# An AdaLN transformer block with attention and a routed feed-forward part on one core: order of weight loads, row stores, ranking and the first feed-forward batch's preparation

## The reference, cut to what matters

```python
def attn(x, Wq, bq, Wk, bk, Wv, bv, temperature):      # b=8, t=1024, d=512, 16 heads of 32
    q = (x @ Wq + bq).reshape(b, h, dh, t)             # k and v alike
    attn = softmax(einsum('bhdt,bhds->bhts', k, v) * temperature)
    return einsum('bhdt,bhts->bhds', q, attn).reshape(b, t, d)

def ffn(hidden, w_router, W1, b1, W2, b2):             # F = 2048
    scores = einsum('bsd,d->bs', hidden, w_router)
    top_scores, top_idx = top_k(scores, 512)           # half of the 1024 tokens of a batch
    selected = take_along_axis(hidden, top_idx)
    processed = gelu(selected @ W1 + b1) @ W2 + b2
    return hidden.at[top_idx].add(sigmoid(top_scores) * processed)

sa, ca, ga, sb, cb, gb = (silu(c) @ wmod) split in six  # |ga|, |gb| at least 0.25
h = layernorm(x) * (1 + ca) + sa
x = x + ga * attn(h, ...)
h = layernorm(x) * (1 + cb) + sb
x = x + gb * ffn(h, ...)
```

## Time and profile before

| what | value |
|---|---|
| profiled execution, own time | 2431.43 us |
| its span | 2429.7 us |
| median of the timed runs | 2440.17 us |
| PE busy | 2272.0 us (94%) |
| DVE busy | 1903.2 us (78%) |
| ACT busy | 1477.5 us (61%) |
| POOL busy | 1367.7 us (56%) |

### The profile page before, as it was taken

One profiled execution on the slowest core, in us unless ns is written; L12 is line 12 of the kernel. 1 busy time (PEld: TensorE's weight loads), 2 busy tenths in 40 slices (PEclk: granted clock), 3 DMA queues, 4 the chain that ended last, 5 costly groups with the idle time before them and its releaser, 6 DMA issues.

```text
span 2429.7 us, 41301 instructions
## 1 busy us (share of the span) xinstructions
PE 2272.0 (94%) x12772; PEld 886.5 (36%) x12772; DVE 1903.2 (78%) x2806; ACT 1477.5 (61%) x2616; POOL 1367.7 (56%) x1205
## 2 busy tenths in 40 slices
PE   7999999999999999999999999877689999999996
PEld 2333333333333333333333333222244444444443
DVE  5899999999999999999999999988444543553432
ACT  1788888888888888878888888767211111111110
POOL 4566676667666666667666675553344452443531
PEclk9999999999999999999999999999899999999998
DMA  6233333232333334233333334223312012011100
GB/s 212 69 91 78 78 87 85 68 96 67 81 95 75 74 77 101 68 79 83 79 81 90 77 71 101 64 60 110 108 44 66 22 48 62 28 61 44 54 25 18
DMA packets 123771, 180.83 MB, mean 74 GB/s; under 512 B 44112, under 2 KB 44112, under 8 KB 123480
## 3 DMA queue, kind: packets, MB, share of 16 engines
q1 hardware_dynamic: 113760, 152.30, 25.0%
q0 software_dynamic: 9728, 25.23, 3.4%
HBM read 67.17 MB, written 43.16 MB: 45 GB/s over the span
## 4 chain that ended last, share of the span: by engine, by line
PE 65%; DVE 16%; issue 9%; POOL 4%; ACT 3%; DMA 1%; SPq 1%; DVEq 0%; POOLq 0%; ACTq 0%
PE sc L552 13%; PE sc L741 13%; PE acc L599 13%; PE sc L728 12%; DVE nmax L976 9%; PE pj L562 8%; PE pj L574 5%; POOL x L1314 3%; DVE qn L1037 2%; ACT probs L804 2%; DVE stats L1019 1%; PE sc L585 1%; PE sc L614 1%; DVE rinv L1032 0%; DMA room<-in_L_ffn_W 0%
## 5 line engine op out<-in xcount | busy, mean ns | idle before, releaser
L804 ACT ACTIVATE probs<-sc,nmax 128x1024 f32<-128x1024 f32 x1024 | 1136.7, 1115 | 272.5 <-DVE nmax L976 254.8
L976 DVE TENSOR_REDUCE nmax<-sc 128x1 f32<-128x1024 f32 x1024 | 1212.1, 1215 | 57.0 <-PE sc L552 51.4
L599 PE MATMUL acc<-probs,qn 128*32 128x512 f32 x4136 | 554.6, 609 | 3.3 <-DVE qn L1037 2.3
L878 ACT ACTIVATE probs<-sc,b_col 128x512 f32<-128x512 f32 x128 | 87.8, 687 | 552.2 <-PE sc L728 552.1
L562 PE MATMUL pj<-room 128*128 128x512 f16 x1536 | 395.3, 381 | 0.4 <-ACT qT L794 0.4
L741 PE MATMUL sc<-room,probs 128*128 128x512 f16 x1536 | 354.7, 381 | 26.8 <-DVE probs L1165 26.8
L552 PE MATMUL sc<-room 128*128 128x512 f16 x1024 | 309.4, 384 | 40.7 <-ACT probs L804 24.1
L552 PE MATMUL sc<-stacks 128*128 128x512 f16 x1024 | 309.6, 384 | 38.3 <-ACT probs L804 37.7
L1163 DVE CAST probs<-probs 128x512 f16<-128x512 f32 x128 | 62.5, 489 | 356.3 <-ACT probs L878 356.1
L741 PEld LDWEIGHTS sc<-room,probs 128*128 128x128 f16 x1536 | 150.3, 98 | 209.8 <-DVE probs L1165 27.6
L562 PEld LDWEIGHTS pj<-room 128*128 128x128 f16 x1536 | 150.1, 98 | 188.4 <-issue 8.9
(11 more groups left out here) (147 smaller groups left out, 2361.1 us busy)
## 6 DMA issues: line engine op xcount, KB each, us to landing
room<-room SPq DMA_DIRECT2D x512, 64.0 KB, 2.0
stacks<-room SPq DMA_DIRECT2D x512, 64.0 KB, 2.0
h_rows<-hbuf SPq DMA_DIRECT2D x132, 128.0 KB, 2.4
out<-base SPq DMA_DIRECT2D x132, 128.0 KB, 2.6
room<-in_L_attn_x SPq DMA_DIRECT2D x96, 128.0 KB, 2.5
rows<-mod_rows SPq DMA_DIRECT2D x32, 256.0 KB, 4.0
room<-in_L_ffn_W SPq DMA_DIRECT2D x8, 1024.0 KB, 6.1
probs<-in_L_wmod SPq DMA_DIRECT2D x4, 1024.0 KB, 7.8
```

Of the source, the lines that this page charges most:

```text
L599: mm = nc.tensor.matmul(acc[at:at + DH, :], qn[:, (p // 2) % 2, p % 2, h2, :], probs[:, (2 * p + h2) % PROBS, half * D:(half + 1) * D], st ...
L804: nc.scalar.activation(probs[:, u % PROBS, :], slot(g, ring_at(p, h2)), ACT.Exp, bias=nmax[:, u % PROBS:u % PROBS + 1], accum_out=rsum[:, ...
L878: nc.scalar.activation(g32[:, f % 2, :], ff[f % 2], ACT.Gelu_apprx_tanh, bias=b1_col[:, f:f + 1], scale=1.0 / WS).then_inc(gelu_done, 1)
L976: nc.vector.tensor_reduce(nmax[:, u % PROBS:u % PROBS + 1], slot(g, ring_at(p, h2)), AX.X, ALU.max, negate=True).then_inc(max_done, 1)
```

## The change

Five things move; no arithmetic is added or taken away.

1. SP: loads 4 and 5 are issued ahead of the wait for `post_done` and the last eight row stores.
2. ACT: `high_part(1)` goes from pair 8 to pair 11 of the last group, `high_part(2)` from pair 12 to behind the group's last exponential, `high_part(4)`, `high_part(5)` and the exponential of the last scores one block later each (blocks 3, 5 and 6).
3. DVE: the ranking of batch 0 is cut in two steps per tile (`count_before` and `count_above`) on pairs of their own; `find_slots` comes at pair 4 of group 30 (the third group of the last batch), which was at pair 8.
4. POOL: two of the eight `store_kept` DMAs go ahead to right after the layer norm of that group.
5. Last group: the list of batch 0 is taken at pair 2 instead of pair 1 of DVE's order, behind one more row maximum; the transposes stand at pairs 6, 9, 12 and 14 (`KEPT_AT`) instead of 8, 10, 12 and 14, `kept_high` one pair behind them and `kept_low` two pairs (the last one a single pair).

```diff
             load_scores(1)
+            for j in range(4, 6):
+                load_weights(j)
             sp.wait_ge(post_done, NG + 1)
             store_rows(NG - 1, (NG - 1) % 2)
-            for j in range(4, 6):
-                load_weights(j)
             sp.wait_ge(s_dot, 2 * NG + 2)
             store_scores(B - 1)
...
+        KEPT_AT = (6, 9, 12, 14)
...
-                            if p >= NQ and p % 2 == 0:
-                                cc = (p - NQ) // 2
+                            if p in KEPT_AT:
+                                cc = KEPT_AT.index(p)
...
-                        if end and p == 8:
+                        if end and p == 11:
                             high_part(1)
-                        if end and p == 12:
-                            high_part(2)
-                        if end and p > NQ and p % 2 == 1:
-                            kept_high(0, 0, (p - NQ) // 2, aux[0])
+                        if end and p - 1 in KEPT_AT:
+                            kept_high(0, 0, KEPT_AT.index(p - 1), aux[0])
...
             body(LAST, True)
+            high_part(2)
             act.wait_ge(s_d, 1)
...
                     if first and f == 0:
                         high_part(3)
-                    if first and f == 2:
+                    if first and f == 3:
                         high_part(4)
-                    if first and f == 4:
+                    if first and f == 5:
                         high_part(5)
-                    if first and f == 5:
+                    if first and f == 6:
                         act.wait_ge(s_dot, 2 * NG + 2)
...
-                if g == 0 and p == 14:
-                    count_above(nc, dve, r, 1, only)
+                if g == 0 and p in (8, 12):
+                    count_before(nc, dve, r, 1 + (p - 8) // 4, only)
+                if g == 0 and p in (10, 14):
+                    count_above(nc, dve, r, 1 + (p - 10) // 4, only)
+                if g == 1 and p in (0, 4, 8, 12):
+                    count_before(nc, dve, r, 3 + p // 4, only)
+                if g == 1 and p in (2, 7, 10, 14):
+                    count_above(nc, dve, r, 3 + p // 4, only)
...
+                if g == 2 and p == 0:
+                    count_before(nc, dve, r, 7, only)
+                if g == 2 and p == 2:
+                    count_above(nc, dve, r, 7, only)
                 if g == 2 and p == 4:
-                    count_above(nc, dve, r, 7, only)
-                if g == 2 and p == 8:
                     dve.wait_ge(s_tok, 3)
                     find_slots(nc, dve, r, r.tokens[:, 0:TB, :], only)
...
                         row_max(b, g, p, 0)
+                        if end and p == 2:
+                            numbers(0, 0)
+                        if end and p - 2 in KEPT_AT[:CC - 1]:
+                            kept_low(0, 0, KEPT_AT.index(p - 2), aux[0])
...
                     normed_before(b, g)
+                    if last and g == GB - 2:
+                        wait_alone(r.s_slot, 1)
+                        store_kept(nc, r, sel_rows, range(0, TB // 4))
                     behind_qn(b, g, 4)
...
                     if last and g == GB - 2:
-                        wait_alone(r.s_slot, 1)
-                        store_kept(nc, r, sel_rows, range(0, TB // 2))
+                        store_kept(nc, r, sel_rows, range(TB // 4, TB // 2))
```

More of the change, by code:

```diff
@@ L75, with count_before @@
 RANK_STEPS = 4
-def count_above(nc, dve, r, t, count):
+def count_before(nc, dve, r, t, count):
     own = t * P
@@ L86, in count_above @@
                                 accum_out=r.before[:, t:t + 1]).then_inc(r.s_cmp, 1)
+def count_above(nc, dve, r, t, count):
+    own = t * P
     nc.vector.tensor_scalar(r.cmp_out[:, own:T], r.srow[:, own:T], r.s8[:, t:t + 1], 0.0, ALU.is_gt, ALU.add,
@@ L842, in body @@
                             evac_q((g + 1) % 2, (p - 13) // 2, n2 + (p - 13) // 2 + 1)
-                        if last and g == 1 and p == 1:
+                        if last and g == 1 and p == 0:
                             act.wait_ge(s_dot, 2 * (NG - 3))
@@ L1082, in rank_first @@
                     count_above(nc, dve, r, 0, only)
-                if g == 0 and p == 14:
-                    count_above(nc, dve, r, 1, only)
+                if g == 0 and p in (8, 12):
[6 more added lines that the diff above has]
+                    count_above(nc, dve, r, 3 + p // 4, only)
                 if g == 1 and p == 1:
-                    count_above(nc, dve, r, 2, only)
-                if g == 1 and p == 4:
                     weights(slice(0, LAST * TB), 1)
[L1089 to L1096, removed]
+                if g == 2 and p == 0:
+                    count_before(nc, dve, r, 7, only)
+                if g == 2 and p == 2:
+                    count_above(nc, dve, r, 7, only)
                 if g == 2 and p == 4:
-                    count_above(nc, dve, r, 7, only)
-                if g == 2 and p == 8:
                     dve.wait_ge(s_tok, 3)
@@ L1130, in body @@
                             rank_first(g, p)
-                        if end and p == 1:
-                            numbers(0, 0)
                         if end and p == 7:
                             low_part(0)
-                        if end and p > NQ and p % 2 == 1:
-                            kept_low(0, 0, (p - NQ) // 2, aux[0])
+                        if end and p == PAIRS - 1:
+                            kept_low(0, 0, CC - 1, aux[0])
             with dve.Fori(0, B - 1) as b:
@@ L1155, in count_tile @@
                         dve.wait_ge(r.s_srow, count(16, 16))
+                    count_before(nc, dve, r, t, count)
                     count_above(nc, dve, r, t, count)
```

## The result

The changed kernel takes 2416.92 us (median of 4 runs, 2414.27 to 2418.5), the kernel before 2438.86 us (4 runs, 2436.71 to 2441.03), timed together with it: ratio 0.9909, 95% interval 0.9892 to 0.9926. It is 21.9 us faster, 18 to 26 by the interval. Forecast: 24.9 us less, 2415.3 us, with a range of 2405 to 2427. The forecast time was taken from a median of 2440.17 us over three runs; the fourth brought that down by 1.3 us, so the saving was missed by 3.0 us and the time by 1.6 only.

What follows compares the result with a forecast made beforehand. PE, busy 94% of the span, was taken as the bound, winnable only where it stands still; DVE paces attention. 24.2 - 6.2 + 6.9 + 0 = 24.9 us off 2440.2 gives 2415.3 us, range 2405 to 2427.

Steps and rivals of the forecast that it cites:

- A: First feed-forward batch: early loads 4 and 5 and later high part 4 remove PE's stall and half clock; 24.2 us gained.
- B: First feed-forward batch: load 6 becomes late, delaying split 8 and block 12's transposes; 6.2 us lost, between 4.3 and 8.3.
- C: Last attention group: earlier list and fewer DVE waits for kept rows and scores; 6.9 us gained, bounds 2.6 to 9.7.
- D: Batch 0's ranking in half tiles: worth 0, only tie counts could shift; 5.4 us lost to 3.2 saved.
- the stall goes: At ff2(3): gelu 3 no longer stands behind high part 4; 22.5 us idle and 2.6 us half clock saved.
- Rival 1: First feed-forward batch: load 6 is in time, B = 0; saving 31.1, 2409.1 us; chance 0.14.
- Rival 2: Attention: DVE keeps the pace, C = 3.8, all tie counts long, D = -5.4; saving 16.4, 2423.8 us; chance 0.21.
- Rivals 3 and 4: Load 4 still late, saving 6.0, chance 0.06; or four-byte writes delay load 6, 10 us slower, chance 0.02.
- signs of being right: No gap at ff2(3), full clock, load 6 14 to 18 us, ACT wait 9, ff2(8) gap 3, transposes 11.7, list wait below 1.5.
- signs of being wrong: PE gap at the last group's pair 6, ACT wait for load 4, or attention ending less than 3 us earlier.

Runs made afterwards that it cites:

- x_loads: Kernel before with only loads 4 and 5 early and the high parts and last exponential of the first feed-forward batch reordered; 2423.2 us, ratio 0.994.
- x_norank: Changed kernel with the ranking and its scatters put back as before; 2418.77 us, ratio 0.9921.
- f_, g_ and c_ kernels: Changed kernel with further edits to its first feed-forward batch or to POOL's last operations; ratios 0.9887 to 0.9926 to the kernel before.
- c_pool: Changed kernel with POOL's four last operations on h and base cut to 32 of 512 columns, work left out; 2410.52 us, ratio 0.9887.
- f_score: Changed kernel with loads 6 and 7 issued ahead of the store of the last scores; 2414.51 us, ratio 0.9908.
- g_low4: Changed kernel with low part 4 behind the split of gelu 4 on DVE instead of ahead of it; 2414.43 us, ratio 0.9907.
- g_best: Changed kernel with low part 4 behind split 4, high part 6 behind gelu 8, loads 6 and 7 ahead of the scores; 2412.87 us, ratio 0.9898.
- f_tile: Changed kernel with the first tile of batch 1's ranking one block later on DVE; 2417.4 us, ratio 0.9926.
- x_last: Kernel before with only the last attention group's edits: list one row maximum later, KEPT_AT, high parts 1 and 2 moved; 2435.36 us, ratio 0.9991.
- before_again: Kernel before, unchanged, profiled a second time; 2437.95 us.
- f_both: Changed kernel with batch 1's first ranking tile one block later and high part 6 behind gelu 8; 2412.83 us, ratio 0.9907.

## Why the prediction was right

The time was forecast at 2415.3 and measured at 2416.92; the saving was 21.9 us and not 24.9. Part of the nearness is luck: one loss was missed in A, and it hid part of the loss counted in B. Term by term, against the means of the table:

| term | forecast, us | measured, us | from |
|---|---|---|---|
| A and B | 24.2 - 6.2 = 18.0 | 17.7 | III: 101.3 (four without the early loads) - 83.6 (x_loads, x_norank, after) |
| C | 6.9 | 5.4 | II: 78.1 (before twice, x_loads) - 72.7 (after, f_, g_ and c_ kernels) |
| D | 0 | -2.3 | I: 141.7 (five without it) - 144.0 (nine with it) |
| sum | 24.9 | 20.8 | medians: 21.9 |

**A** held. No gap of 22.5 us, load 4 landed in the 4.9 us of a quiet load, high part 4 did not wait, and the first ff1 was 1.05 us late where I had 0.9. But its cover for DVE was not seen: the stall had also kept POOL's last h and base operations away from DVE. The step "the stall goes" looked at what PE, ACT and SP would meet next and left out DVE beside POOL. c_pool and x_loads show it: splits 3 and 4 late, gaps of 0.66 and 2.80 us and 1.6 us of lower clock, some 5 us in all. In c_pool, where that loss is gone and load 6 is late by little, III is 24.2 us shorter (101.3 to 77.1), A's own size, though part of POOL's work is left out there.

**B** held in its mechanism and not in its place. Load 6 landed after 16.2 us (I took 16; 14 to 18), the four-byte writes being 7.5 of them (f_score). It was issued 34.2 us behind the last products and not 32.8, since the store of the last scores waited for DVE's last router product, which ended at 1725.28. But the gap came at ff2(4) instead of ff2(8), ACT waited 3.5 us and not 9, because PE reached that place 5 us later. The two losses hide each other: with high part 6 or the scores moved the changed kernel gains only 1.4 us; with low part 4 moved only, it gains nothing; with all three 4.4 (all in stretch III). Taken behind g_low4, where PE is in time, the load's price is 85.00 - 79.64 = 5.4 us, beside the 6.2 of the forecast. So the sum of A and B came out (18.0 and 17.7) partly since the loss that I had missed took the place of the one that I had counted. The Trainium skill, "SBUF — State Buffer", section "Who interferes with whom", was cited for the tie counts only. The same section says that casts and copies in their 2-port modes contend with GpSimd too, and that of two that contend the second one to issue is held until the first is through. The cast, the copy and the subtraction agree (each ends 0.02 to 0.6 us behind a POOL operation, and c_pool has them short), though no row shows the mode. The section should have been asked of every DVE instruction that the change puts beside POOL.

**C** was mis-sized by 1.5 us, inside its bounds (2.6 to 9.7). The earlier list brought what it should: from the 62nd residual to the next one 27.12 us instead of 30.51, 3.4 beside 3.8. The rest of the group gave 45.37 instead of 47.19 to 47.62, 2.1 beside 3.1; in the kernels with the same edits it lies between 43.29 (f_tile) and 46.70 (f_score), so a single execution does not fix it. The sign that I had named for it, a wait of less than 1.5 us for the list, did not come (3.69): I had subtracted the list's gain and the row maximum from 4.53 us and left out that DVE itself arrives earlier. From the residual to DVE's wait it takes 20.60 us, before 22.03, with one row maximum more. Most of that is a router product, which stood beside POOL's base in before and, with the ranking's edits, hardly does now (two rows of before, two of after):

```profile
1626.12 2.38 POOL L1347 TENSOR_TENSOR base<-base,x 128x1024 f32<-128x1024 f32 x1
1626.17 2.89 DVE L1005 SCALAR_TENSOR_TENSOR dot_out<-hbuf,router_row 128x512 bf16<-128x512 f32 x1
...
1630.43 2.36 POOL L1353 TENSOR_TENSOR base<-base,x 128x1024 f32<-128x1024 f32 x1 [0.30 <-issue]
1632.48 0.86 DVE L1010 SCALAR_TENSOR_TENSOR dot_out<-hbuf,router_row 128x512 bf16<-128x512 f32 x1
```

In x_last, with the ranking as before, that router product takes 3.06 us. So DVE still waits for the list, and the gain is real all the same.

**D** was put at nothing and measured at 2.3 us lost, inside the bounds (-5.4 to 3.2). The step that failed is that the tie counts would stay short: the longest was bounded by 1.43 us and now takes 2.36:

```profile
L96 DVE SCALAR_TENSOR_TENSOR tie_out<-srow,s,earlier x64: 340/349/2364, 1490.8 to 2266.1; 128x128 bf16<-128x128 f32 x64
```

Over batch 0's eight tiles, tie counts took 10.3 us and not 6.0, and the places of dropped tokens (`drop`, in `find_slots`) 2.25 and not 1.25, while the four router products of stretch I became cheaper, 3.9 and not 5.9 (two more, behind it, 1.75 and not 3.78): different instructions met POOL's.

The 2.3 us are a mean over a wide spread, I being 140.08 to 143.98 in the five kernels without the halves and 143.96 to 144.05 in the nine with them. The spread is not in DVE's work. In stretch I DVE is busy for 135.3 to 135.6 us in the five and 139.1 to 139.4 in the nine, 3.9 us more; it stands still for 4.7 to 8.4 us in the five and 4.6 to 4.9 in the nine. What varies are waits of 1.2 us for PE's scores, one in before, three in x_loads, four in x_last, none in before_again and x_norank. So the halves cost 3.9 us of DVE's work, of which the others spend 1.5 on average waiting. Why the number of these waits changes between executions of the same instructions is open.

**Rivals.** Rival 1 (load 6 in time) is refuted for the changed kernel: 16.2 us and an ACT wait. Rival 2 had its direction right, as C and D gave less, 3.1 us instead of its -1.6. Rivals 3 and 4 show nothing in the trace. Of the signs of being right: 0.66 us before ff2(3) where no gap was forecast; clock 1.00 until 1724 and 0.62 behind it; load 6 in 16.2 us; an ACT wait of 3.5 us and not 9; no gap at ff2(8); 10.69 us before the transposes beside 11.7. Of the signs of being wrong, there is no gap at pair 6 and no wait for load 4. The third, the attention part ending less than 3 us earlier, came by a hair: I and II together are 216.7 us in the eight kernels that have the whole change in them, 219.5 in the three that have none of it there, 2.9 us less.

## What to carry to other kernels

A stall shelters what runs beside it: before taking it away, list what the other engines do in it, GpSimd against VectorE above all, and ask which instructions will stand there when the engines come earlier. Two late inputs on one path do not add up, and undoing one alone shows little; undo them together, and price each from the version in which the other is gone. Compare profiled executions by stretches between fixed points: the spans here said 14.6 us where the medians said 21.9.

## What the runs showed of the hardware

- VectorE beside GpSimd: a 512-column cast 2.21 instead of 0.43 us, a subtraction 2.72 instead of 0.69, a low part 4.43 instead of 2.28, even a copy of 8 columns 2.31 instead of 0.28. GpSimd's four operations end at 1713.03 (half of the 4.84), 1715.45, 1718.21 and 1720.64; VectorE's cast, subtraction, copy and tie count beside them at 1713.25, 1716.00, 1718.23 and 1720.79. With GpSimd's operations cut to 32 columns cast, subtraction and copy are short. The comparison beside the last of them took 1.28 us as without GpSimd.
- A load of 1 MB behind the store of 1024 scores of 4 bytes lands after 14.1 to 17.9 us, in front of it after 7.8 and 8.7 (g_best, f_score), quiet after 4.9 to 5.1.
- TensorE's clock after short gaps: a gap of 2.80 us was followed by a block at the lower level (4.37 us, granted clock 0.62), and so was one of 2.31 in f_both; in f_tile one of 2.31 and in x_norank one of 2.79 were not (2.75 us per block). The gap alone does not say.
- Executions of the same instructions differ ahead of the changed part: the 57th residual starts at 1470.49 to 1478.28 in 14 executions. Taken from every eighth residual to the next, each of the first six batches of the loop takes 198.3 to 201.5 us, the same batch up to 3.0 us more in one execution than in another; the seventh takes 196.3 to 196.4 in all of them.
